# Four scratch writes issued ahead of one input load in a queue of an attention kernel

## The chip, the cores and the metric

The kernel runs on one core of a Trainium2 chip. The metric is the device time of one execution in microseconds, and the time before is the median of three runs. Work is spread over TensorE (PE, with its weight loads as PEld), VectorE (DVE), ScalarE (ACT), GpSimd (POOL) and the DMA engines; SyncE (SP) issues nearly all the transfers, in the order in which they are written down. Each of these engines works off its own instructions in order, and they wait for each other through semaphores.

## The reference, cut to what matters

```python
B, S, E, H = 4, 512, 256, 16                 # as drawn here; HD = 16
qkv = x @ Wqkv.T + bqkv
attn = softmax(q @ k.T / sqrt(HD))           # per batch and head, 512 x 512
mod = attn * coh; mod = mod / (mod.sum(-1) + 1e-8)   # coh: a small gated MLP on [x, cond]
mod = (1 - fi) * mod + fi * fa               # fa: one softmax row per batch, from cond
x = x + (mod @ v) @ Wout.T + bout
x = x + quaternion_rotation(x * gate)        # a fixed 256 x 256 linear map
```

## The kernel before

**Batches, halves, groups, steps.** The four batches are worked through one after the other. The 16 heads of a batch are two *halves* of 8 heads, each half two *groups* of 4 heads. One step of the main loop on PE does one block of scores for the row maxima (`scores_for_max(n)`, L990, here called S(n): two matmuls), and, 12 steps later (`LEAD`), one block of transposed scores (`scores`, L1003) from which ACT takes exponentials (L513), and every second step eight matmuls with the values (`weigh_values`, L1018). Eight steps make a group, 32 a batch. DVE reduces each S block to negated row maxima (L660). The side work (projections q, k, v, the coherence MLP `coh0` and `coh1`, outputs) is cut into jobs that a hand-written table assigns to steps. In batch 0 they are: `dq0`, `dk0`, `q0` before step 0, `k0` at step 0, `dq1` at 1, `dk1` at 2, `q1` at 3, `k1` at 4, `v0` at 5, `v1` at 6, `cond` and `norms` at 7, `coh0` at 8, `max0` and `fpre` at 9. S(n) stands ahead of the jobs of step n.

**The stack.** For accuracy q and k are split into a high and a low part, `qk_hi` (written by ACT, L536) and `qk_lo` (by DVE, L676), each with one buffer a side (side 0 is q, side 1 is k). A job for one half gives 128 features of one side. `write_qk(half)` stores the four parts in a DRAM scratch, and `read_stack(half)` reads them back by six DMAs into one of three slots of `stack`, in the layout that the scores need. `read_stack` waits for both sides' writes (`side_written`) and for the rows of maxima of earlier groups (`max_loaded`). ACT can't write the next `qk_hi` of a side before the last writes of that side have landed (a wait for `side_written` in `qk_high`).

**The first half.** The first four heads, used by S(0) to S(7), don't go through the scratch: the jobs `dq` and `dk` multiply the raw x by repeated weights (L806) and put the result in the stack directly. They read `x_raw`, and `dk1` is the last job that does. The other four heads of half 0 come by the scratch, and S(8) is the first instruction that needs them. S(16) is the first that needs half 1. The rows of maxima of a group (`max0` for the first: a transpose on PE L849, a copy on ACT L554, a small DMA L558) are loaded after the group's S blocks. `read_stack(1)` waits for those of `max0`.

**x.** `x_raw` is one buffer. `load_x(1)` overwrites the first batch's x by the second's, and so waits for the low part of x (`x_lo_done`) and for `dk1` to be filled on PE. ACT splits x for the second batch at step 4, between the evacuations of `q1` and `k1`, and POOL makes its low part after that (L372).

**SyncE's order.** After 12 loads of weights and constants it is `load_x(1)`, `write_qk(0)`, `read_stack(0)`, `write_qk(1)`, `read_stack(1)`, then a loop over the batches. The first x comes by ACT's queue.

Of the kernel before, what the change touches and what calls it, by code (L numbers as in the profile page):

```python
# [119 lines left out]
def wait(eng, sem, value):  # L120
    if value > 0:
        eng.wait_ge(sem, value)
# [7 lines left out]
def build(nc, x, xT, wdirT, wqkvT, wc1T, wc2T, we2T, woutT, w64, rows, small, cols, pe_table, identity, out):  # L130
    with ExitStack() as ctx:
# [119 lines left out]
        def wait_job(eng, job):  # L251
            wait(eng, job_filled, PLACE[job] + 1)
# [8 lines left out]
        def _(sp):  # L261
# [17 lines left out]
            def load_x(b):  # L279
                wait(sp, x_lo_done, b)  # L280
                if b == 1:

                    wait_job(sp, ("dk1", 0))
                sp.dma_start(x_raw[:, :, :], xT.rearrange("(k p) (b s) -> b p k s", p=P, b=B)[b]).then_inc(ld_x, 16)
# [5 lines left out]
            def write_qk(half):  # L290
                dst = scratch[half].rearrange("n p s -> p n s")
                for side in range(2):
                    wait(sp, q_hi_done, 2 * half + side + 1)
                    sp.dma_start(dst[:, 1 + side], qk_hi[:, side].bitcast(F32)).then_inc(side_written[side], 16)
                    wait(sp, q_lo_done, 2 * half + side + 1)
                    sp.dma_start(dst[:, 3 * side], qk_lo[:, side].bitcast(F32)).then_inc(side_written[side], 16)

            def read_stack(half):
                slot, turn = slot_of(half)
                for side in range(2):  # L300
                    sp.wait_ge(side_written[side], 32 * (half + 1))

                wait(sp, max_loaded, 16 * max(2 * half - 2, half))

                wait(sp, t_filled, 16 * (half - HALF_SLOTS + 1))
                first = 2 if half == 0 else 0
                if half < HALF_SLOTS:
                    sp.wait_ge(ones_done, 1)
                src = scratch[half].rearrange("n (r a h) s -> a r n h s", r=HD, a=2)
                for a in range(2):  # L310
                    for t, (q_part, k_part) in enumerate(((1, 3), (1, 2), (0, 2))):
                        dst = stack[64 * a + t * HD:64 * a + (t + 1) * HD, :, 4 * slot + first:4 * slot + 4, :]
                        sp.dma_start(dst.bitcast(F32), src[a][:, q_part:k_part + 1:k_part - q_part, first:4, :]  # L313
                                     ).then_inc(stack_loaded[slot], 16)
# [6 lines left out]
            def store(b):  # L321
                for half in range(2):
                    sp.wait_ge(out_ready, 2 * b + half + 1)
                    sp.dma_start(out.rearrange("b (i p) e -> b p i e", p=P)[b][:, 2 * half:2 * half + 2, :],
                                 y[:, b % 2, 2 * half:2 * half + 2, :]).then_inc(out_stored, 16)

            load_x(1)
            write_qk(0)
            read_stack(0)
            write_qk(1)  # L330
            read_stack(1)
# [767 lines left out]
```

## Time and profile before

| | |
|---|---|
| median of 3 runs | 307.35 us (306.35 to 308.05) |
| span of the profiled execution | 302.4 us |
| what lies around the span, against the median | 4.95 us |
| PE busy | 272.4 us (90%) |
| DVE, ACT, POOL busy | 197.7, 176.2, 157.9 us |
| mean granted TensorE clock | 0.977 of full speed |
| DMA | 31.11 MB, q1 (SyncE's) 50.9% of the 16 engines' span |

The span runs from the first to the last instruction. The page gives no device time for the profiled execution alone, so its own time is taken as its span and the 4.95 us around it. The rows further down are read as start, duration, what; a releaser stands in brackets behind an idle time.

### The profile page before, as it was taken

What the parts mean: (1) busy time and instruction counts of PE and PEld (TensorE: products, weight loads), DVE (VectorE), ACT (ScalarE), POOL (GpSimd) and SP (SyncE); (2) the same over time, 40 slices, a digit from 0 to 9 for tenths busy, and PEclk for the clock granted to TensorE, in tenths of its full rate; (3) what the DMA queues carried; (4) which work ended last, traced back from release to release, by engine and by line L of the source; (5) the groups of instructions that cost most, each with busy time, mean ns of one, the idle gap of its engine ahead of it and who ended that gap; (6) DMA issues with size and microseconds to landing.
All of it is one profiled execution on the core that took longest, in us unless ns stands there. A gap on an engine that the chain in (4) does not pass through costs nothing.

```text
span 302.4 us, 4278 instructions
## 1 busy us (share of the span) xinstructions
PE 272.4 (90%) x1579; PEld 130.0 (43%) x1579; DVE 197.7 (65%) x227; ACT 176.2 (58%) x214; POOL 157.9 (52%) x143
## 2 busy tenths in 40 slices
PE   8999397598979999999899999999999988899973
PEld 6447244233534444444444454446444433344422
DVE  6485355556777677887577668785876778864113
ACT  3224034456667768676448677674667666655760
POOL 3933639998199999993003069960000399900000
PEclk9999687989999999999999999999999999999999
DMA  7717839739773934399318933695159500101002
GB/s 240 214 44 217 192 53 121 175 61 120 138 245 52 125 37 152 98 117 173 126 69 109 109 83 122 96 121 171 54 86 121 90 2 4 33 3 69 1 0 72
DMA packets 16020, 31.11 MB, mean 103 GB/s; under 512 B 2232, under 2 KB 8248, under 8 KB 14656
## 3 DMA queue, kind: packets, MB, share of 16 engines
q1 hardware_dynamic: 15168, 30.15, 50.9%
q10 hardware_dynamic: 832, 0.69, 0.8%
q8 instruction: 13, 0.21, 0.3%
q14 instruction: 7, 0.06, 0.1%
HBM read 20.21 MB, written 10.49 MB: 102 GB/s over the span
## 4 chain that ended last, share of the span: by engine, by line
PE 59%; DVE 18%; DMA 13%; issue 4%; SPq 2%; POOL 1%; ACT 1%; DVEq 0%; ACTq 0%; POOLq 0%
PE o_ps L1018 15%; DVE maxima L660 14%; PE job_ps L794 12%; PE pair_ps L990 11%; PE pair_ps L1003 9%; DMA stack<-qk_scratch 6%; PE job_ps L908 4%; DMA stack<-max_rows 3%; DVE qk_lo L676 2%; DMA w_raw<-wqkvT 2%; DMA qk_scratch<-qk_lo 2%; SPq L313 1%; PE pair_ps L882 1%; PE job_ps L849 1%; PE pair_ps L794 1%
## 5 line engine op out<-in xcount | busy, mean ns | idle before, releaser
L660 DVE TENSOR_REDUCE maxima<-pair_ps 128x2 f32<-128x1024 f32 x128 | 155.5, 1222 | 69.1 <-PE pair_ps L990 69.1
L513 ACT ACTIVATE probs<-pair_ps 128x1024 f32<-128x1024 f32 x128 | 130.8, 1025 | 65.6 <-PE pair_ps L1003 64.9
L990 PE MATMUL pair_ps<-stack 48*128 48x512 f32 x256 | 64.5, 500 | 8.2 <-DMA stack<-qk_scratch 7.6
L1018 PE MATMUL o_ps<-probs,vals 128*32 128x512 f32 x512 | 69.0, 612 | 0.8 <-ACT probs L513 0.8
L1003 PE MATMUL pair_ps<-stack 49*128 49x512 f32 x256 | 57.1, 444 | 9.8 <-DVE maxima L660 7.0
L990 PEld LDWEIGHTS pair_ps<-stack 48*128 48x128 f32 x256 | 24.2, 186 | 56.9 <-issue 40.0
L389 POOL TENSOR_TENSOR vals<-v_new,row 128x256 f32<-128x256 f32 x16 | 11.3, 733 | 48.5 <-ACT v_new L545 48.2
L1003 PEld LDWEIGHTS pair_ps<-stack 49*128 49x128 f32 x256 | 24.4, 187 | 28.3 <-DVE maxima L660 18.8
L488 POOL TENSOR_TENSOR prod<-amap,x_tok 128x1024 f32<-128x1024 f32 x12 | 28.6, 2382 | 0.9
L372 POOL TENSOR_TENSOR x_lo<-x_raw,x_hi 128x1024 fp32r<-128x1024 f32 x3 | 7.1, 2375 | 32.9 <-ACT x_hi L519 32.8
L490 POOL TENSOR_TENSOR y<-y,prod 128x1024 f32<-128x1024 f32 x8 | 19.1, 2382 | 0.6
L1018 PEld LDWEIGHTS o_ps<-probs,vals 128*32 128x32 f32 x512 | 10.1, 108 | 21.0 <-issue 18.1
L794 PE MATMUL job_ps<-x_hi,w_hi 128*128 128x512 f32 x40 | 15.6, 474 | 0.2
L794 PE MATMUL job_ps<-x_hi,w_lo 128*128 128x512 f32 x40 | 13.4, 419 | 0.0
L794 PE MATMUL job_ps<-x_lo,w_hi 128*128 128x512 f32 x40 | 13.2, 412 | 0.0
L536 ACT ACTIVATE qk_hi<-job_ps,col 128x512 fp32r<-128x512 f32 x12 | 8.3, 689 | 7.8 <-PE job_ps L794 7.8
L569 ACT ACTIVATE hT<-job_ps,percond 128x512 f32<-128x512 f32 x8 | 5.5, 689 | 12.2 <-PE job_ps L794 12.2
L908 PE MATMUL job_ps<-wf,oT 128*128 128x256 f32 x48 | 11.9, 390 | 0.3
L866 PE MATMUL job_ps<-ident,o_raw 128*128 128x128 f32 x64 | 10.5, 286 | 1.3 <-ACT o_raw L588 0.6
L908 PEld LDWEIGHTS job_ps<-wf,oT 128*128 128x128 f32 x48 | 8.6, 189 | 3.2 <-issue 2.3
L866 PEld LDWEIGHTS job_ps<-ident,o_raw 128*128 128x128 f32 x64 | 6.7, 140 | 7.7 <-issue 2.8
L493 POOL TENSOR_TENSOR y<-y,prod 128x1024 f32<-128x1024 f32 x4 | 9.5, 2378 | 0.3
(134 smaller groups left out, 297.2 us busy)
## 6 DMA issues: line engine op xcount, KB each, us to landing
stack<-qk_scratch SPq DMA_DIRECT2D x42, 256.0 KB, 8.9
qk_scratch<-qk_hi SPq DMA_DIRECT2D x16, 256.0 KB, 5.4
qk_scratch<-qk_lo SPq DMA_DIRECT2D x16, 256.0 KB, 5.8
x_tok<-x SPq DMA_DIRECT2D x4, 512.0 KB, 14.3
out<-y SPq DMA_DIRECT2D x8, 256.0 KB, 2.2
x_raw<-xT SPq DMA_DIRECT2D x3, 512.0 KB, 5.9
fa_now<-fa_rows SPq DMA_DIRECT2D x4, 256.0 KB, 7.7
stack<-qk_scratch SPq DMA_DIRECT2D x6, 128.0 KB, 4.7
```

What stands on the lines that cost most here:

```text
L389: nc.gpsimd.tensor_tensor(vals[:, :, g * HG:(g + 1) * HG, 0:HD], src, bias.unsqueeze(1).to_broadcast([P, IT, HG, HD]), ALU.add).then_inc(v ...
L488: chain(nc.gpsimd.tensor_tensor(dst, a, s, ALU.mult))
L490: chain(nc.gpsimd.tensor_tensor(y_b, y_b, tmp, ALU.add))
L493: nc.gpsimd.tensor_tensor(y_b, y_b, tmp, ALU.add).then_inc(y_done, 1)
L513: nc.scalar.activation(probs[:, t % 4, :, :], ps[:, :, :], ACT.Exp, scale=SCALE).then_inc(exp_done, 1)
L660: nc.vector.tensor_reduce(maxima[:, gg % 2, :, pair, i], pair_ps[SLOT["S", u]][:, :, :], AX_X, ALU.max, negate=True).then_inc(s_reduced, 1)
L794: ins = nc.tensor.matmul(out_ap, stat(a, k), mov(c, k), start=(n == 0), stop=(n == 3 * KT - 1))
L866: ins = nc.tensor.transpose(bank(job)[:, i * P:(i + 1) * P], o_raw[:, i * P:(i + 1) * P], ident[:, :])
L908: ins = nc.tensor.matmul(ps[:, tile * E:(tile + 1) * E], oT[:, k, i * P:(i + 1) * P], wf[:, k, :], start=(k == 0), stop=(k == KT - 1))
L990: ins = nc.tensor.matmul(pair_ps[SLOT["S", u]][:, a, :], stack[64 * a:64 * a + ROWS, 0, p, i * P:(i + 1) * P], stack[64 * a:64 * a + ROWS, ...
L1003: ins = nc.tensor.matmul(pair_ps[SLOT["T", t]][:, a, :], stack[64 * a:64 * a + ROWS + 1, 1, p, j * P:(j + 1) * P], stack[64 * a:64 * a + R ...
L1018: ins = nc.tensor.matmul(o_ps[h * VW:(h + 1) * VW, :], vals[:, j, gg % G * HG + h, :], probs[:, (2 * k + h // 2) % 4, h % 2, :], start=(j ...
```

## The change

SyncE issues the four writes of half 0 before the load of the second batch's x; each keeps its waits. Nothing else is touched.

```diff
+            write_qk(0)
             load_x(1)
-            write_qk(0)
             read_stack(0)
             write_qk(1)
             read_stack(1)
```

## Rows read from the trace of the kernel before

**Rows 1.** The page: granted TensorE clock in 40 slices; chain by engine and line.

```profile
PEclk9999687989999999999999999999999999999999
...
PE 59%; DVE 18%; DMA 13%; issue 4%; SPq 2%; POOL 1%; ACT 1%; DVEq 0%; ACTq 0%; POOLq 0%
PE o_ps L1018 15%; DVE maxima L660 14%; PE job_ps L794 12%; PE pair_ps L990 11%; PE pair_ps L1003 9%; DMA stack<-qk_scratch 6%; PE job_ps L908 4%; DMA stack<-max_rows 3%; DVE qk_lo L676 2%; DMA w_raw<-wqkvT 2%; DMA qk_scratch<-qk_lo 2%; SPq L313 1%; PE pair_ps L882 1%; PE job_ps L849 1%; PE pair_ps L794 1%
```

**Rows 2.** That chain in order of time: start us, us, what.

```profile
17.87 1.93 PE o_ps L806 x4
...
21.79 5.33 DMA qk_scratch<-qk_lo
...
29.41 5.78 DMA stack<-qk_scratch
...
39.56 0.22 PE o_ps L849
...
40.10 1.83 DMA stack<-max_rows
...
44.30 13.37 DMA stack<-qk_scratch
```

**Rows 3.** Timeline of SyncE: start us, us, instruction.

```profile
19.88 0.38 SPq L284 DMA_DIRECT2D x_raw<-xT  x1
...
27.17 2.67 SPq L313 DMA_DIRECT2D stack<-qk_scratch  x6
...
42.08 2.65 SPq L313 DMA_DIRECT2D stack<-qk_scratch  x6
```

**Rows 4.** Timelines of DVE and of ACT, the splits of q and k.

```profile
16.71 0.74 DVE L676 SCALAR_TENSOR_TENSOR qk_lo<-pair_ps,col,qk_hi 128x512 fp32r<-128x512 f32 x1
...
13.09 0.69 ACT L536 ACTIVATE qk_hi<-pair_ps,col 128x512 fp32r<-128x512 f32 x1 [1.43 <-PE pair_ps L794]
...
25.96 0.69 ACT L536 ACTIVATE qk_hi<-pair_ps,col 128x512 fp32r<-128x512 f32 x1 [5.37 <-PE job_ps L794]
26.55 1.05 ACT L519 ACTIVATE x_hi<-x_raw 128x1024 fp32r<-128x1024 f32 x1
```

**Rows 5.** Timeline of PE, its waits from step 7 to step 16.

```profile
28.63 0.50 PE L990 MATMUL pair_ps<-stack 48*128 48x512 f32 x2 [0.67 <-DVE maxima L660]
...
29.77 0.46 PE L958 MATMUL pair_ps<-n_diag,n_ones 64*128 64x128 f32 x2
35.23 0.79 PE L990 MATMUL pair_ps<-stack 48*128 48x512 f32 x2 [4.99 <-DMA stack<-qk_scratch]
...
49.42 0.33 PE L842 MATMUL job_ps<-ident,ez 128*128 128x128 f32 x1 [1.74 <-DVE qk_lo L676]
...
57.72 0.51 PE L990 MATMUL pair_ps<-stack 48*128 48x512 f32 x2 [2.57 <-DMA stack<-qk_scratch]
```

**Rows 6.** Stretches: PE, PEld, DVE, ACT, POOL busy us, PEclk, DMA share, GB/s.

```profile
14.00:20.90 6.90, 6.90 (x22) 3.13 (x21) 5.45 (x7) 2.24 (x3) 4.12 (x9) 1.00 0.00 0
...
22.00:23.00 1.00, 1.00 (x6) 0.69 (x5) 1.00 (x2) 0.00 (x0) 0.00 (x0) 1.00 0.95 244
...
28.00:34.00 6.00, 1.61 (x12) 1.38 (x12) 3.49 (x4) 2.05 (x8) 6.00 (x6) 0.88 0.99 146
33.00:38.50 5.50, 3.27 (x8) 2.10 (x8) 1.23 (x1) 0.00 (x0) 2.50 (x3) 0.50 0.63 197
```

**Rows 7.** DMA issues: KB each, us from issue to landing (the x load, a 256 KB store).

```profile
x_raw<-xT SPq DMA_DIRECT2D x1, 512.0 KB, 4.6
...
out<-y SPq DMA_DIRECT2D x4, 256.0 KB, 2.2
```

**Rows 8.** The chain again, later: S blocks, a projection, a slow load of maxima.

```profile
94.00 1.60 PE job_ps L794 x6
...
97.26 0.45 PE pair_ps L990 x2
...
139.74 5.90 DMA stack<-max_rows
```

## The prediction

> **What bounds the kernel now.** I read the page's chain first. PE carries 59% of it and DVE 18%, in the ping-pong of score blocks and their reductions; but 13% is DMA, and the largest piece of that is the read of the stack from the scratch, 6% [rows 1]. The chain in order of time shows that this 6% is just two transfers, both early: 5.78 us that end at 35.19 and 13.37 us that end at 57.67 [rows 2]. So I read the start engine by engine. PE stands 4.99 us before S(8), up to 35.23, and 2.57 us before S(16), up to 57.72, both for the stack [rows 5]. The granted clock is below full only in the first 68 us, the first nine slices [rows 1], and no other read of the stack stands on the chain. Whatever comes earlier in this start should therefore bring all the rest earlier.
>
> What is behind the first wait? The chain goes back over the six reads (issued from 27.17) to the last write of half 0 (issued at 21.79, landed 5.33 us later at 27.12), to the x load at 19.88 and to `dk1` on PE, which ends at 19.80 [rows 2, 3]. That last link is only an order in a queue. The data of the writes doesn't need `dk1`: the first high part is done at 13.09 + 0.69 = 13.78, and the last low part (k's) at 16.71 + 0.74 = 17.45 [rows 4]. Between 14 and 20.9 us the DMA engines move nothing [rows 6]. SyncE stands in front of the x load with finished writes behind it.
>
> **The writes, moved ahead.** Four issues (from 20.26 to about 22.2, so some 0.45 us each) no longer follow the x load. Each goes out when its part is ready; the last, at about 17.5 us, is 4.3 us earlier than 21.79. How long it takes to land is not in the trace for this position, since there all four writes had 512 KB of x ahead of them and each other. From below: the 256 KB stores of the output at the end, with nothing in flight, land in 2.2 us [rows 7]. From above: 5.33 us, the very write in the crowd [rows 2]. The engines are idle here and the earlier three writes are spread over 4 us, so the store is the nearer row; I take 2.4 us, a landing at 19.9 (bounds 19.7 and 22.8), against 27.12.
>
> **The x load, moved behind four waits.** SyncE passes the four writes at about 17.95, and waits then for `dk1` as before, so the load is still issued at 19.88. It is the only transfer that the four issues are moved past, and it loses nothing: its cover is the 1.9 us that SyncE still waits for PE. Were that cover gone, each issue would cost it 0.45 us, and x isn't urgent: ACT took it up at 26.55 [rows 4] and it had landed at 24.5 (4.6 us, rows 7).
>
> **The six reads.** They follow the x load in the queue. Their own wait is satisfied at 19.9, so they are issued from 20.3 to 23.0, against 27.17 to 29.84. From first issue to last landing they took 35.19 - 27.17 = 8.0 us [rows 2, 3]. But now x moves in front of them. In the trace the data of x begins to flow at 20.9, 1 us after its issue, and 524 KB at the 244 GB/s of the microsecond after 22 [rows 6] are 2.15 us. So the engines are busy with x from 20.9 to about 23.1; the reads alone would have started at 21.35, so x pushes them back by 1.7 us. They land at 20.3 + 8.0 + 1.7 = 30.0. Bounds: 28.3, if x fits beside them; and, with the write at its upper bound, 22.8 + 8.0 = 30.8 (x is then out of the way), and 0.5 for x standing partly in front even so: 31.3.
>
> At this place the page "DMA: Bandwidth & Descriptors" of the Trainium skill, section "Queues, rings and completion order", speaks against a part of the gain: on each DMA engine descriptors are consumed in the order of the ring, so reads issued behind x stand behind its bytes. By that rule the landing is 30.0, and without it 28.3. No row here shows the two side by side, but the reads at 28 to 34 us run at a mean DMA share of 0.99 [rows 6], so there is no room beside them either way.
>
> **S(8).** PE gets there earlier too, but little. `norms` ended at 30.23. The one wait between is the 0.67 us of S(7) on DVE's reduction [rows 5], which stood behind q1's low part on DVE, which stood behind q1's high part: ACT could write it only at 25.96, when q's writes had landed [rows 4]. Now those land at about 18, q1's split is done by about 24.4, and the 0.67 us goes: PE arrives at 29.56. (ACT then waits for x up to about 24.5, and takes k1 after it, done at 26.3 against 28.2.) S(8) runs at 30.05 instead of 35.23: 5.2 us. If the reads landed before 29.56, the gain would be 5.67 and no more.
>
> **The clock.** In the pause before S(8) the granted clock falls from 1.00 to 0.50, the lower of the two levels, and is at 0.50 throughout from 33 to 38.5 us [rows 6]. PE had been idle since 30.23 [rows 5]; the stretch from 28 to 34 still has 0.88 as its mean, so the fall comes at about 32.6 (1.00 to there and 0.50 for the rest gives 0.88). So S(8), `coh0` and S(9) ran slow: 39.56 - 35.23 = 4.33 us from S(8) to `max0` [rows 2, 5]. At the upper level the same two blocks and projection are 0.45 + 1.60 + 0.45 = 2.50 us [rows 8]. With a pause of 0.5 us I expect no fall, for PE's pause of 0.67 us was followed by none. That is 1.83 us more, so `max0` runs at 32.6 instead of 39.56: 7.0 us.
>
> **The second read.** `read_stack(1)` waits for the rows of `max0`, loaded 1.83 us after 40.10 [rows 2]. ACT's copy ahead of it may be held 0.1 us by the tanh of `coh0`, so of the 7.0 I keep 6.9. The writes of half 1 can't hold it: behind the reads of half 0 they move their 1 MB by about 32. The reads go out at 35.2 instead of 42.08, and take as before 57.67 - 42.08 = 15.6 us; they land at 50.8. Does PE wait there as before? It arrived 57.72 - 2.57 - 35.23 = 19.9 us after S(8); less 1.83, that is now 48.1, and waits 2.6 us. S(16) runs at 50.8 instead of 57.72.
>
> **Behind it** everything hangs on PE, or on SyncE waits for rows of maxima, and moves along; the loads of weights are all over before 14 us. POOL's long work starts from the mean and variance of `fpre` at step 9 and shifts likewise, since the jobs ahead of it on POOL hang on x and `v0`, which come no later than now.
>
> The sum: 5.2 + 1.8 - 0.1 = 6.9 us. The profiled execution: span 302.4 - 6.9 = 295.5, with 4.95 around it 300.45. As the 4.95 was taken against the median, that is also 307.35 - 6.9. I say 300.4.
>
> **Rivals.**
> (a) The clock falls all the same, because the pause is longer (reads at their upper bound, 31.3) or because it looks at PE otherwise than I think. Then the 1.83 us stays and the gain is 5.2 down to 35.23 - 31.3 = 3.9: 302.2 to 303.4. For it: the clock is below full in slices five to seven and nine [rows 1], and before one of them (the seventh, 45 to 53 us) PE paused only 1.74 us [rows 5]. Chance 0.2.
> (b) Gain given back later. Rows of maxima, x_tok and the stack share the DMA engines, and a row of maxima once took 5.90 us [rows 8]; a small shift of POOL's work against PE's could make another such wait, or an extra fall of the clock. To cancel 5.4 us or more it would need three of the kind (a fall costs about 1.8). Time 306 to 308. Chance 0.05.
> (c) The other sign: x lands late. With reads crowding it, x reaches ACT late; ACT works in order, so `k1`, and DVE's low part of it, wait behind the split of x, and `norms` on PE, just ahead of S(8), needs k1's bank read. From x's landing to that are 1.05 + 0.69 + 0.74, about 2.5 us. It becomes slower than now when x lands after 32.3, 12.4 us after issue; at 35 it would cost 2.7 us: about 310. Against it: x is issued first and took 4.6 us with four writes behind it. Chance 0.03.
> (d) The change does nothing, because the landing of the reads hangs on something else than their issue: 307.35, chance 0.02. The idle DMA engines up to 20 us speak against it.
> (e) More than said: the reads land by 28.3 and S(8) gains the full 5.67, so 7.4 in all: 299.9; inside my case.
>
> My case 0.70; (a) 0.20. Its range: 299.3 to 301.5, from (e) and 0.6 us of scatter below, and from a read at 30.8 without a fall above. The runs before span 1.7 us. With (a) taken in up to 303.4 and a fall of the clock that no longer happens after S(16) (the ninth slice, at 0.8 [rows 1]; a gain of up to 1.8 that I don't count) partly below: 298.9 to 303.6. About 0.5% (1.5 us) can be told from no change: faster 0.91, the same 0.05, slower 0.04.
>
> **What would show it.** The fourth write issued near 17.5, x still near 19.9, the first read at 20.3 and S(8) at about 30 with a pause under 1 us; PEclk 1.00 from 30 to 40 us; `max0` at 32.6; the second read from 35.2; S(16) at 50.8, still with a wait of some 2.6 us. I would be wrong if the reads were issued after 22 us, if x in front of them cost more than 1.7 us, if the clock fell at 32, or if the last 250 us were not of the same length as before.

## The result, and the profile after

The changed kernel took 300.03 us at the median (297.24 to 302.98, 4 runs), against 307.48 us (306.35 to 308.05, 4 runs) before, with a ratio of 0.9733 (95% interval 0.9675 to 0.979). The forecast was 300.4 us. The profiled execution of the changed kernel took 297.24 us with a span of 295.4 us, 7.0 us less than the span of before. Each ratio in this document compares the fast runs only (those not more than 1.5% above the fastest of the same kernel), while the medians are of all runs, so the two can differ.

SyncE's timeline of the changed kernel, start us, us, instruction:

```profile
13.53 0.33 SPq L294 DMA_DIRECT2D qk_scratch<-qk_hi  x1
15.17 0.33 SPq L296 DMA_DIRECT2D qk_scratch<-qk_lo  x1
15.56 0.41 SPq L294 DMA_DIRECT2D qk_scratch<-qk_hi  x1
17.20 0.32 SPq L296 DMA_DIRECT2D qk_scratch<-qk_lo  x1
19.60 0.38 SPq L284 DMA_DIRECT2D x_raw<-xT  x1
20.09 2.73 SPq L313 DMA_DIRECT2D stack<-qk_scratch  x6
...
35.17 2.65 SPq L313 DMA_DIRECT2D stack<-qk_scratch  x6
```

The writes now go out one by one as the parts get ready, and the x load has not moved (19.88 before, in a trace whose PE is 0.27 us later from the first block on). The first reads are issued at 20.09 instead of 27.17, the second at 35.17 instead of 42.08 [rows 3]. What they release is seen on PE's timeline:

```profile
28.76 0.47 PE L958 MATMUL pair_ps<-n_diag,n_ones 64*128 64x128 f32 x2
30.13 0.50 PE L990 MATMUL pair_ps<-stack 48*128 48x512 f32 x2 [0.91 <-DMA stack<-qk_scratch]
...
32.59 0.28 PE L849 MATMUL o_ps<-ident,maxima 128*16 128x128 f32 x1
...
50.12 0.80 PE L990 MATMUL pair_ps<-stack 48*128 48x512 f32 x2 [3.32 <-DMA stack<-qk_scratch]
```

The pause of 4.99 us before S(8) has become 0.91 us, and S(16) comes 7.60 us earlier [rows 5]. The chain in order of time has two links other than [rows 2]. The last write of half 0 is gone from it, so the x load and the reads now follow `dk1` directly; and ACT's copy of the rows of `max0` now stands behind ACT's tanh for `coh0` (L569):

```profile
17.58 1.93 PE o_ps L806 x4
...
22.40 7.69 DMA stack<-qk_scratch
...
30.63 1.61 PE job_ps L794 x6
...
32.27 0.69 ACT hT L569
...
33.20 1.83 DMA stack<-max_rows
...
37.40 12.67 DMA stack<-qk_scratch
```

The projection behind S(8) takes 1.61 us, as at full clock [rows 8]. Stretches of the changed kernel (PE, PEld, DVE, ACT, POOL busy, PEclk, DMA share, GB/s) show where the clock stands:

```profile
30.00:40.00 10.00, 9.48 (x53) 5.04 (x53) 6.60 (x7) 3.36 (x6) 8.25 (x13) 1.00 0.56 106
49.00:56.00 7.00, 5.88 (x22) 2.04 (x22) 2.48 (x3) 2.38 (x4) 6.77 (x3) 0.51 0.37 138
60.00:290.00 230.00, 215.85 (x1339) 98.28 (x1337) 158.69 (x190) 152.18 (x178) 113.34 (x67) 1.00 0.49 90
```

The fall in the pause before S(8) is gone; a fall in the pause before S(16) remains. It now lasts 6.8 us, against 3.4 behind S(16) in the kernel before.

S(16) comes 7.60 us earlier and the span is 7.0 us shorter. The distance between the two traces changes in three places behind S(16). The longer low stretch brings it down to 7.23 us. At 138 us it goes up to 7.58, because a late load of rows of maxima held the kernel before for 1.26 us and this one for 0.91. The third place costs 0.60 us, and PE's timeline shows it:

```profile
194.56 0.50 PE L1003 MATMUL pair_ps<-stack 49*128 49x512 f32 x2
...
201.74 0.51 PE L1003 MATMUL pair_ps<-stack 49*128 49x512 f32 x2 [0.45 <-DMA stack<-max_rows]
```

Between these two L1003 blocks lie 7.18 us. In the kernel before the same two stood at 202.14 and 208.72, 6.58 us apart, with no wait for the rows of maxima:

```profile
202.14 0.50 PE L1003 MATMUL pair_ps<-stack 49*128 49x512 f32 x2
...
208.72 0.51 PE L1003 MATMUL pair_ps<-stack 49*128 49x512 f32 x2
```

The chain of the changed kernel has a 5.09 us load of those rows here. It is the mechanism of rival (b), at 0.60 us. Some 0.27 us of the 7.0 are not the change's, for PE is that much earlier already before the first instruction that was moved can matter.

### The profile page after: what moved, and what is told of

The parts are those of the page before. It is cut to its first block, busy times and chain, and to the rows that moved or that the text cites. A ratio compares the mean times of both kernels' runs of the same rounds, so it can differ in the third digit from the quotient of the medians.

```text
span 295.4 us, 4278 instructions
## 1 busy us (share of the span) xinstructions
PE 269.7 (91%) x1579; PEld 128.4 (43%) x1579; DVE 198.0 (67%) x227; ACT 176.2 (60%) x214; POOL 157.7 (53%) x143
## 4 chain that ended last, share of the span: by engine, by line
PE 60%; DVE 17%; DMA 14%; issue 4%; SPq 2%; ACT 1%; POOL 1%; DVEq 0%; ACTq 0%; POOLq 0%
PE o_ps L1018 16%; DVE maxima L660 13%; PE job_ps L794 11%; PE pair_ps L990 11%; PE pair_ps L1003 10%; DMA stack<-qk_scratch 7%; DMA stack<-max_rows 5%; PE job_ps L908 4%; DVE qk_lo L676 2%; DMA w_raw<-wqkvT 2%; SPq L313 1%; PE pair_ps L882 1%; PE job_ps L866 1%; PE job_ps L849 1%; PE pair_ps L794 1%
## 5 line engine op out<-in xcount | busy, mean ns | idle before, releaser
L1003 PE MATMUL pair_ps<-stack 49*128 49x512 f32 x256 | 57.2, 445 | 9.4 <-DVE maxima L660 6.5
L1003 PEld LDWEIGHTS pair_ps<-stack 49*128 49x128 f32 x256 | 24.5, 187 | 28.2 <-DVE maxima L660 18.5
L794 PE MATMUL job_ps<-x_hi,w_hi 128*128 128x512 f32 x40 | 14.7, 448 | 0.2
L794 PE MATMUL job_ps<-x_hi,w_lo 128*128 128x512 f32 x40 | 12.6, 396 | 0.0
L794 PE MATMUL job_ps<-x_lo,w_hi 128*128 128x512 f32 x40 | 12.6, 396 | 0.0
L488 POOL TENSOR_TENSOR y<-amap,x_tok 128x1024 f32<-128x1024 f32 x4 | 9.5, 2377 | 0.3
```

Of the source, the lines that this page charges most:

```text
L488: chain(nc.gpsimd.tensor_tensor(dst, a, s, ALU.mult))
L794: ins = nc.tensor.matmul(out_ap, stat(a, k), mov(c, k), start=(n == 0), stop=(n == 3 * KT - 1))
L1003: ins = nc.tensor.matmul(pair_ps[SLOT["T", t]][:, a, :], stack[64 * a:64 * a + ROWS + 1, 1, p, j * P:(j + 1) * P], stack[64 * a:64 * a + R ...
```

## The experiments

### The x load behind the reads

```diff
             write_qk(0)
-            load_x(1)
             read_stack(0)
+            load_x(1)
```

> SyncE's order is writes of half 0, reads of half 0, then the x load. Theory (x's bytes stand in front of the reads and cost them 1.7 us; but x has a deadline through ACT's order): the reads are issued from about 19.25 and land at about 27.3, and x lands near 29.3, behind them. ACT then splits x up to 30.4, k1 follows, DVE's low part of k1 is done near 31.8 and the reductions of steps 6 and 7 behind it; S(8) waits for those and runs near 33, the clock falls in the pause, max0 near 37 against 32.6, so about 4.4 us slower than the changed kernel: 304.4. Rival (x does not share with the reads, its landing is as before after the issue, 4.6 us): x lands at 26.6 and S(8) runs near 29.5, the whole 0.5 us or more faster than the changed kernel.

Measured: 304.01 us at the median of 10 runs (302.55 to 309.94), before 306.32 (19 runs), ratio 0.996 (0.991 to 1.0011), which can't be told from the kernel before. x lands at 29.4, ACT splits it at 29.44, and the rest follows in ACT's order. ACT, DVE and PE of this kernel, each from its timeline:

```profile
29.44 1.06 ACT L519 ACTIVATE x_hi<-x_raw 128x1024 fp32r<-128x1024 f32 x1 [6.56 <-DMA x_raw<-xT]
30.40 0.67 ACT L536 ACTIVATE qk_hi<-pair_ps,col 128x512 fp32r<-128x512 f32 x1
...
31.10 0.75 DVE L676 SCALAR_TENSOR_TENSOR qk_lo<-pair_ps,col,qk_hi 128x512 fp32r<-128x512 f32 x1 [5.21 <-ACT qk_hi L536]
...
31.91 0.79 PE L958 MATMUL pair_ps<-n_diag,n_ones 64*128 64x128 f32 x2 [2.39 <-DVE qk_lo L676]
33.13 0.80 PE L990 MATMUL pair_ps<-stack 48*128 48x512 f32 x2 [0.43 <-DVE maxima L660]
```

Each row hangs on the one above. From x's landing to `norms` are 2.5 us, as rival (c) was priced, and the durations of the last two rows are those of the lower clock. S(8) at 33.13 and `max0` at 37.44 (expected: 33 and 37) fit the theory. So nearly all of the gain is gone: a late x is a real danger in this kernel. In the changed kernel it lands at about 24.5, early enough.

### The same, with x split later on ACT

```diff
-                if n % PER_BATCH == 4 and n // PER_BATCH < B - 1:
+                if n % PER_BATCH == (7 if n < PER_BATCH else 4) and n // PER_BATCH < B - 1:
                     x_high(n // PER_BATCH + 1)
```

> As the run before, but ACT splits the second batch's x after the evacuations of k1, v0 and v1 (step 7 instead of step 4). Theory: with ACT's order out of the way the late x costs nothing, the reads land near 27.3, and S(8) runs when PE gets there, near 29.2, without a pause for the stack; the rows of max0 are copied near 32.3 instead of 32.9 and S(16) comes 0.6 to 0.9 us earlier than in the changed kernel: about 299.4. Rival (what held S(8) was not ACT's order but x's landing by another way, such as POOL's low part of x): it stays near 33, as in the run before.

Measured: 299.60 us (298.59 to 300.11, 4 runs), ratio 0.9831 (0.9732 to 0.9931) to the same before. The x load is issued at 22.27 and split at 29.02, S(8) runs with no pause (its first matmul at 28.89, beside those of `norms`), and S(16) at 49.35 instead of 50.12. The theory held: x lands at 29.0 here and at 29.4 in the run before, so what made the late x dear was ACT's order alone. A gain over the changed kernel is not shown. S(16) is 0.8 us earlier than in that kernel's first trace, but `max0`, at 31.65, lies within the 31.5 to 32.6 of the three traces whose start is the changed kernel's (below), and the medians can't resolve 0.8 us.

### Only q's two writes ahead

```diff
-            write_qk(0)
+            write_qk(0, (0,))
             load_x(1)
+            write_qk(0, (1,))
             read_stack(0)
```

(`write_qk` takes the sides to write as its second argument here; that edit is left out above.)

> Only q's two writes of half 0 stand ahead of the x load, k's two behind it. Theory (the last of the four writes sets the reads; x ahead of it delays it): q1's high part on ACT is early as in the changed kernel (21.6), but the last write is issued near 20.9 and lands near 24.6, so the reads go out from 24.6 and land near 32.6; S(8) there, after a pause of 3.4 us, the clock falls, and max0 is near 36.9: about 2.6 us faster than before, 304.8. Rival (the gain came from q's buffers being free earlier and the 0.67 us of S(7)): nearly all of the gain of the changed kernel, about 300.5.

Measured: 305.33 us (300.12 to 306.86, 10 runs), ratio 0.9953 (0.9844 to 1.0062), which doesn't tell it from no change. The trace tells more. PE, from its timeline:

```profile
27.61 0.50 PE L991 MATMUL pair_ps<-stack 48*128 48x512 f32 x2
...
28.76 0.47 PE L959 MATMUL pair_ps<-n_diag,n_ones 64*128 64x128 f32 x2
33.59 0.80 PE L991 MATMUL pair_ps<-stack 48*128 48x512 f32 x2 [4.36 <-DMA stack<-qk_scratch]
```

S(7) is as early as in the changed kernel, so q's part of the change does free ACT and DVE. But the reads go out at 25.56 (expected 24.6), because the last write is issued at 20.54 with x in front of it. S(8) waits 4.36 us, in which the clock falls, and S(16) comes at 55.73, 2.0 us earlier than in the first trace of before and 1.2 earlier than in its second. The early q buffers by themselves are worth next to nothing: the last of the four writes sets the reads.

### x by ACT's queue

```diff
             write_qk(0)
-            load_x(1)
             read_stack(0)
...
+                if n == 3:
+                    wait(act, x_lo_done, 1)
+                    wait_job(act, ("dk1", 0))
+                    act.dma_start(x_raw[:, :, :],
+                                  xT.rearrange("(k p) (b s) -> b p k s", p=P, b=B)[1]).then_inc(ld_x, 16)
```

> The changed kernel, but the second x is loaded by ACT's queue, after ACT has evacuated dk1 (issue near 20.3), and SyncE goes straight from the writes of half 0 to the reads. Theory (the two queues share the same 16 DMA engines, so x and the reads slow each other by x's 2.2 us in all, whichever queue it is in): the reads are issued from 19.3 and land near 29.4, x lands later than 24.5, near 26, S(8) near 29.5, within 1 us of the changed kernel. Rival (a queue of its own takes x out of the reads' way): the reads land near 27.5 and S(8) goes with no pause at 29.2.

Measured: 299.02 us (297.74 to 300.07, 4 runs), before 307.35 (7 runs), ratio 0.976 (0.9681 to 0.9839). Here the reads go out from 19.88, and the last of them lands at about 29.3, 7.2 us after its issue. x lands at 25.8, 5.6 us after its issue. From first issue to last landing the reads take 9.4 us, against 7.8 to 8.2 in the three traces with x behind them, and x takes 5.6 us, against 4.5 to 4.9 in the changed kernel. Both are slower side by side, so the two share the engines here too, and a queue of its own takes nothing out of the reads' way. S(8)'s first matmul starts at 29.50, with the last of `norms`, 1.3 us after S(7). The changed kernel's first trace has 2.5 us there and its second 1.2, so this order is not shown to be better or worse.

### The clock by itself: filled pauses

In four kernels PE does unneeded matmuls into the bank that the next S block will overwrite, just ahead of its wait for the stack. Each such matmul shows as two in the trace. First the kernel before, with 20 of them before S(8):

```diff
+FILL = {8: 20}
...
                 elif u % 16 == 0 or u == 8:
+                    if u in FILL:
+                        slot_free(("S", u))
+                        for n in range(FILL[u]):
+                            nc.tensor.matmul(pair_ps[SLOT["S", u]][:, 0, 0:P], n_ones[:, :], n_ones[:, :],
+                                             start=True, stop=True)
                     pe.wait_ge(stack_loaded[slot], 96 * (turn + 1))
```

> The kernel before with 20 unneeded matmuls (64x128 by 64x128) on PE into the bank of S(8) just ahead of its wait for the stack, so that PE is busy in the pause of 5 us and no wait is taken away. Theory (the fall of the clock in this pause costs 1.83 us by itself): S(8) still near 35.2, clock 1.00 from 30 to 40 us, max0 near 37.7 instead of 39.56, second read 1.8 us earlier, the whole 1.8 us faster: 305.6. Rival (the clock is not what made max0 late, or the gain is lost in the wait before S(16)): S(16) at 57.7 and 307.4.

Measured: 309.11 us (304.70 to 312.57, 4 runs), before 306.32, ratio 1.0186 (1.0013 to 1.0358): slower, though the interval only just leaves out no change. The step itself came as expected: S(8) at 34.97, `max0` at 37.44, which are 2.47 us instead of 4.33, the clock 1.00 from 30 to 40 us; the second read went out at 40.02 instead of 42.08, and S(16) ran at 55.15 instead of 57.72. It was all lost behind S(16). Stretches of this kernel:

```profile
53.00:60.00 7.00, 4.85 (x18) 1.54 (x18) 2.45 (x2) 2.11 (x3) 6.76 (x6) 0.55 0.47 151
60.00:64.00 4.00, 4.00 (x11) 2.32 (x10) 1.23 (x1) 1.29 (x2) 3.84 (x3) 0.50 0.18 39
```

The low stretch there lasts from 53.7 to 64.0, 10.2 us, where the kernel before had 3.4 us. The traced execution took 304.70 us with a span of 302.9, so behind S(16) it lost 3.1 us to the first trace of before. So the 1.83 us of the clock is a true term up to S(16), and my expectation of a gain at the end was wrong. With both pauses of the kernel before filled, `FILL = {8: 20, 16: 12}`:

> The kernel before with unneeded matmuls in both pauses, 20 ahead of S(8) and 12 ahead of S(16). The run with only the first filled had its maxima 2 us earlier but lost more to a fall of the clock of some 10 us behind S(16). Theory (that fall comes from the pause of 3.5 us before S(16)): with it filled too, S(16) near 55.2, clock 1.00 to 65 us, and the whole about 4 us under the kernel before: 303. Rival (filling work ahead of S(8) costs the clock later in any case): 307 or more, with slow stretches further on.

Measured: 310.00 us (309.70 to 312.57, 4 runs), before 305.56 (7 runs), ratio 1.0161 (1.0085 to 1.0237). The theory fell. Stretches, and PE's timeline:

```profile
24.00:30.00 6.00, 5.31 (x37) 4.07 (x36) 2.94 (x5) 3.19 (x5) 1.63 (x1) 1.00 0.66 221
30.00:40.00 10.00, 9.82 (x49) 9.23 (x48) 2.12 (x2) 0.89 (x5) 6.12 (x8) 0.57 0.74 157
...
31.04 8.21 PE L991 MATMUL pair_ps<-n_ones 64*128 64x128 f32 x38 [0.18 <-DVE maxima L661]
```

The clock fell at about 31.4, in the filling, although PE had been busy for 5.31 of the 6 us up to 30; with only the first pause filled it had been busy for 5.42 of them, and the clock stayed up. So the filling ran at the lower level, took 8 us instead of 4.7 and made S(8) itself late, 38.8. A filled pause costs when the clock falls all the same. Now the changed kernel with `FILL = {16: 12}`:

> The changed kernel with 12 unneeded matmuls (64x128 by 64x128, about 2.8 us) on PE into the bank of S(16), in its pause of 3.3 us before S(16). Theory (the pause makes the clock fall, from 49.3 to 55.1 us, and that slows what follows S(16)): S(16) stays at 50.1, clock 1.00 from 49 to 56 us, step 17's max1 near 52.7 instead of 54.9, so 2 us faster than the changed kernel. Rival (as in the filled pause of the kernel before, the clock falls soon after anyhow and longer): no gain, or 1 to 3 us lost.

Measured: 298.28 us (296.49 to 300.44, 4 runs), before 307.35, ratio 0.9741 (0.9638 to 0.9844). The clock is 1.00 from 48 to 60 us. Next to the changed kernel in the same session (below) it is 1.9 us faster at the median, within what both scatter. Last, the late x and split with `FILL = {16: 13}`:

> The x load behind the reads, the split of x at step 7, and 13 unneeded matmuls in the pause before S(16). Theory: as the run with the late split (S(16) at 49.4), and no fall of the clock after it: 2 us below that run, about 297.5. Rival: a fall elsewhere, 299.6 or more.

Measured: 296.66 us (296.43 to 297.31, 4 runs), ratio 0.9688 (0.9624 to 0.9753): the fastest kernel of the study at the median, and all four runs within 0.9 us. Each of them is below every run of the kernel with the same late split and no filling (298.59 to 300.11), though that was in another session. Its stretch around the filling:

```profile
46.00:56.00 10.00, 9.49 (x64) 5.57 (x66) 5.08 (x5) 4.46 (x7) 9.84 (x33) 0.97 0.45 120
```

In the traces of these last two kernels the clock was low for 3.4 us just ahead of the filling (from 42.7 and from 43.2), with PE at work after its pause of 1.74 us. Neither trace of the changed kernel has that fall. It cost nothing, because PE arrived early for S(16) anyhow: where a fall comes counts as much as how long it is.

### Both kernels again

> The changed kernel itself, beside the next three on one chip. Theory (the gain is a fixed shift of 7 us at the start, and the scatter of either kernel is falls of the clock in different places from run to run): 6 to 7 us below the kernel before of the same chip at the median, with runs 4 us apart. Rival (the first comparison had a lucky draw of clocks and the shift is smaller): 3 to 4 us.

Measured: 300.15 us (298.97 to 300.48, 4 runs), before 307.35 (303.96 to 310.88, 7 runs), ratio 0.9791 (0.9705 to 0.9876). The gain repeats, 7.2 us between the medians; the runs lie 1.5 us apart, not 4. The traced execution, 300.03 us with a span of 298.2, is a second look at the start. SyncE and PE, each from its timeline:

```profile
20.50 2.73 SPq L313 DMA_DIRECT2D stack<-qk_scratch  x6
...
28.02 0.50 PE L990 MATMUL pair_ps<-stack 48*128 48x512 f32 x2
...
29.26 0.50 PE L990 MATMUL pair_ps<-stack 48*128 48x512 f32 x1
...
49.94 0.50 PE L990 MATMUL pair_ps<-stack 48*128 48x512 f32 x2 [3.96 <-DMA stack<-qk_scratch]
```

S(8) has no pause here, although this trace starts 0.4 us later than the first. The six reads land at about 29.2, 8.7 us after their first issue, where the first trace had 10.0. The changed kernel with its pause before S(16) filled has the same start and agrees with the second trace: 8.9 us, and S(8) at 29.06 with no pause. Why the first trace's reads took longer is open. S(16) is at 49.94, within 0.2 us of the first trace. Behind it this execution is 3.0 us longer than the first, with a low stretch of 10.2 us (50.6 to 60.9) and another fall in the last slice of the span.

> The kernel before once more, for a second trace of it. Theory (the start is the same in every execution, and the kernel's runs differ by how long and how often the clock falls): S(8) and S(16) within 0.5 us of 35.2 and 57.7, and a span that differs from 302.4 by as much as slow stretches of the clock behind S(16) explain. Rival (the transfers themselves scatter): other times of landing.

Measured: 304.44 us, span 302.5. S(8) at 34.72 after a pause of 4.83 us, S(16) at 56.93 after 2.11. So the start is within 0.8 us of the first trace's, a little more than the 0.5 expected. The second read took 15.2 us from first issue to last landing, where the first trace had 15.6: the transfers scatter too, by some tenths of a microsecond. Its clock, in the page's 40 slices:

```profile
PEclk9999697959999999999999999999999999999999
```

The ninth slice (60.5 to 68 us) stands at 5 where it was 8 [rows 1], a fall twice as long (6.8 us against 3.4), and the span is the same, since S(16) came 0.8 us earlier. Over two traces of each kernel S(16) stands at 57.72 and 56.93 before, and at 50.12 and 49.94 after. The spans are 302.4 and 302.5 before, and 295.4 and 298.2 after, so a single pair of spans gives anything from 4.2 to 7.1 us; the gain is better taken from the medians.

## Why the prediction was right

**The queue.** The last write went out at 17.20 (17.5 forecast), x at 19.60, the reads from 20.09 (20.3). The last write landed in 2.0 us. I took 2.4, between a store's 2.2 [rows 7] and 5.33; the truth lies even under my lower bound, at no consequence, as SyncE still waited for `dk1` until 19.5.

**x in front of the reads.** Forecast 30.0 for the last landing, measured 22.40 + 7.69 = 30.09. This nearness is partly luck. From first issue to last landing the reads took 10.0 us in this trace, and 8.7 and 8.9 in the two others with the same start. With x behind them they took 7.8 to 8.2, and in the kernel before 8.0 and 7.8. So x in front costs between 0.4 and 2.2 us, about 1.1 in the mean, where I said 1.7; the first trace passes the limit of 1.7 that I had set as a sign of being wrong, the other two don't. The direction is right. The page "DMA: Bandwidth & Descriptors" of the Trainium skill, in the section "Queues, rings and completion order", says that each DMA engine takes the descriptors of its ring in order; the trace agrees in that the reads behind x land later. It doesn't single that rule out, since x in ACT's queue slowed them as well (9.4 us). My reading that a DMA share of 0.99 leaves no room was wrong: from 24 to 30 us the share is 1.02 in the first trace and 1.03 in the second, but they move 192 and 234 GB/s.

**S(8) and the clock.** S(8) at 30.13 (30.05), a pause of 0.91 us (0.5), no fall; `max0` at 32.59 (32.6), 2.46 us after S(8) (2.50). In the other two traces S(8) stood at 29.3 and 29.1 with no pause, as in (e), though the reads land at 29.2 and 29.0 and not at 28.3; so the first trace has the smallest gain here. Filling the pause of the kernel before gave the same 2.47 us without any other change, so this term was shown by itself. (I took `max0`'s 39.56 from the chain; PE's timeline has 39.49, so the term is 1.80 rather than 1.83.)

**The second read.** Issued at 35.17 (35.2), landed at 50.07 (50.8): 14.9 us from its first issue where 15.6 were taken. That is scatter and not the change, for the second trace of the changed kernel has 15.5 and that of the kernel before 15.2. It makes S(16) 7.60 us earlier rather than 6.9. PE arrived there at 46.80, not 48.1, and so waited 3.32 us, not 2.6. The kernel before also has a low clock from 49.6 to 53.0, after its pause of 1.74 us. I had used that fall in rival (a), but hadn't seen that it might go as well and bring PE's arrival forward; the reads end last there, so it changed nothing.

**Behind it.** "Moves along" was nearly right: 7.60 us at S(16), 7.0 at the end. From S(16) to the end were 244.7 us before and 245.3 and 248.3 after, so "the same length" holds to 0.6 us in one trace, and in the other the clock broke it. In the first trace the errors (+0.7 at S(16), -0.6 behind it) cancel, and 0.27 us of the shift was there from the start, so 6.9 against 7.0 is partly luck. So is 300.4 against a median of 300.03, with four runs from 297.24 to 302.98. In the range, a read at 30.8 without a fall gives 301.2 and not 301.5; nothing hangs on it.

**What lies around the span.** Here the working was wrong. 4.95 us isn't what lies around: 297.24 - 295.4 is 1.84, the second trace of the kernel before has 1.94, and the pairs of time and span in the other runs are alike. The profiled execution of before must have taken about 304.2 us, a quick one, and the median run of that kernel is some 3 us longer within its span. The sum held because the forecast was a shift taken off a median, and the medians did shift by 7.45 and 7.2 us in two sessions, whatever lies around the span.

**The clock from run to run** was my weakest point. I priced one fall; in truth both traces of the kernel before have three in the first 68 us, the changed kernel's have one there and one of them another clear one at its end, and their length differs from trace to trace. In the 19 runs of the kernel before of the second session, spans from 299.9 to 306.2 us go with mean clocks from 0.983 down to 0.952. Rival (a) occurred in neither trace of the changed kernel, and rival (d) is out.

## What to carry to other kernels

Look in a queue for finished work behind an instruction that waits for something else: here one 512 KB load with a wait held up four writes, then the reads, then a second read, and the gain was the whole shift, since nothing later was tied to absolute time. Before a load is moved back, follow who takes it up in order: x landed at about 24.5 in the changed kernel and had, by my estimate, 1.8 us of slack (`norms` at 28.8 less the 2.5 us from x to `norms` is 26.3). At 29.4 ACT's fixed order turned its lateness into a stall of PE 2.5 us later. And a pause on the critical engine can cost more than its length: 4.99 us of pause came with 1.8 us of slow matmuls behind it. Look at a second trace of the same kernel before a difference of about a microsecond is explained: here the pause before S(8) was 0.91 us in one and nothing in the other.

## What I had not expected of the hardware

The granted clock falls not only in pauses. With 5.31 us of 6 busy up to 30 us it fell at 31.4 and stayed low to about 45. How long it stays low doesn't follow the pause ahead of it: before S(16), pauses of 2.57, 2.11, 3.32, 3.54, 3.54 and 3.96 us went with low stretches of 3.4, 6.8, 6.8, 6.8, 10.2 and 10.2 us. Filling the pause of 3 us went with a gain: of 1.9 us, within the scatter, in the changed kernel, and clearly with the late split, whose four runs lie between 296.43 and 297.31 us. Filling one of 5 us in the kernel before made that kernel slower twice, by 1.6% and 1.9%. What decides between these was not found.
